# Values of two key tiles at a time, paired products in three pieces, and gathers one at a time in a fused attention and mixture-of-experts kernel

## The reference

```python
x = L0_attn_x                                   # (8, 512, 256)
xn = layernorm(x)
# attention, 16 heads of 16: each of q, k, v and the output is a low-rank projection
def holo_linear(x, basis, phase, amp):          # basis (32, 256), phase and amp (256, 32)
    return (x @ basis.T) @ (amp * cos(phase)).T
attn = softmax(q @ k.T * 16 ** -0.5); out = holo_linear(attn @ v, basis_o, phase_o, amp_o)
# feed-forward: 8 experts of width 352, the best 2 of each row, weighted, plus shared experts of width 704
y = sum_e combine[t, e] * (silu(xn @ w_gate[e]) * (xn @ w_up[e])) @ w_down[e]
y = y + (silu(xn @ sw_gate) * (xn @ sw_up)) @ sw_down
return x + out + y
```

## Time and profile before

| | us |
|---|---|
| median of 3 runs | 1055.94 |
| lowest, highest | 1054.34, 1062.08 |
| the profiled execution | 1056.45 |
| its span, first to last instruction | 1054.6 |
| TensorE busy in the span | 931.8 (88%) |
| VectorE busy | 646.0 (61%) |
| ScalarE busy | 568.1 (54%) |
| GpSimd busy | 327.9 (31%) |
| mean granted TensorE clock | 0.926 of full |

### The profile page before, as it was taken

One profiled execution on the slowest core, in us unless ns is written; L12 is line 12 of the kernel. 1 busy time (PEld: TensorE's weight loads), 2 busy tenths in 40 slices (PEclk: granted clock), 3 DMA queues, 4 the chain that ended last, 5 costly groups with the idle time before them and its releaser, 6 DMA issues.

```text
span 1054.6 us, 19404 instructions
## 1 busy us (share of the span) xinstructions
PE 931.8 (88%) x6519; PEld 624.2 (59%) x6520; DVE 646.0 (61%) x978; ACT 568.1 (54%) x892; POOL 327.9 (31%) x305
## 2 busy tenths in 40 slices
PE   5756999999999779898998998998997998998898
PEld 3446999999999624455454455444544544544546
DVE  7778644444434555765774874874875775785653
ACT  5756544444444335554663663663664664665563
POOL 2006422222222060351343253244235235135043
PEclk9856999999999856898998998998998999999899
DMA  9976454222222354445446545545465365453220
GB/s 317 377 253 191 137 164 115 73 71 70 70 70 66 94 146 127 124 119 147 126 117 174 151 111 166 147 129 142 133 154 154 108 169 134 138 122 77 48 63 21
DMA packets 94086, 140.02 MB, mean 133 GB/s; under 512 B 18200, under 2 KB 51488, under 8 KB 92992
## 3 DMA queue, kind: packets, MB, share of 16 engines
q1 hardware_dynamic: 87328, 121.25, 40.5%
q0 software_dynamic: 6480, 17.70, 5.7%
q10 hardware_dynamic: 208, 0.14, 0.0%
HBM read 79.24 MB, written 54.71 MB: 127 GB/s over the span
## 4 chain that ended last, share of the span: by engine, by line
PE 48%; issue 24%; POOL 11%; DVE 9%; ACT 3%; another core or an unknown queue 2%; DMA 2%; SPq 0%; POOLq 0%; ACTq 0%; DVEq 0%
PE bank L1253 7%; PE s_pair L1235 6%; PE st_pair L1235 6%; PE bank L1382 5%; PE bank L1444 4%; PE st_pair L1370 4%; POOL y_b L784 3%; PE bank L1348 3%; POOL h_T L767 3%; PE s_pair L1309 3%; DVE top L1773 2%; PE bank L1243 2%; PE bank L1218 2%; ACT prob L1031 1%
## 5 line engine op out<-in xcount | busy, mean ns | idle before, releaser
L1773 DVE TENSOR_REDUCE top<-s_pair 128x2 f32<-128x1024 f32 x252 | 308.5, 1224 | 144.0 <-PE s_pair L1309 122.7
L1031 ACT ACTIVATE prob<-st_pair 128x1024 f32<-128x1024 f32 x256 | 261.6, 1022 | 217.1 <-PE st_pair L1370 152.5
L767 POOL TENSOR_TENSOR h_T<-h_f,h_T 128x512 fp32r<-128x512 f32 x40 | 51.3, 1283 | 410.7 <-ACT h_T L1013 410.7
L1382 PE MATMUL bank<-prob,v_ones 128*32 128x512 f32 x1024 | 156.4, 637 | 4.6 <-issue 4.3
L745 POOL DMA_INDIRECT xg<-xn_rows,token_of x71 | 82.9, 1168 | 216.6 <-PE bank L1218 164.6
L1348 PE MATMUL bank<-xT_b,w_sh 64*128 64x512 f32 x960 | 129.5, 402 | 15.7 <-DVE h_f L1794 13.4
L1370 PE MATMUL st_pair<-q_rows,k_rows 50*128 50x512 f32 x512 | 126.3, 480 | 14.7 <-ACT prob L1031 7.5
L1309 PE MATMUL s_pair<-k_rows,q_rows 48*128 48x512 f32 x504 | 117.0, 450 | 14.4 <-DVE top L1773 7.4
L1370 PEld LDWEIGHTS st_pair<-q_rows,k_rows 50*128 50x128 f32 x512 | 51.0, 191 | 122.8 <-ACT prob L1031 78.0
L1348 PEld LDWEIGHTS bank<-xT_b,w_sh 64*128 64x128 f32 x960 | 91.1, 188 | 43.4 <-DVE h_f L1794 22.3
L1253 PE MATMUL bank<-w_exp,c_hT 128*128 (+1 forms) x639 | 94.2, 292 | 1.0 <-ACT c_y L957 1.0
(11 more groups left out here) (233 smaller groups left out, 1163.7 us busy)
## 6 DMA issues: line engine op xcount, KB each, us to landing
qk_rows<-qk_hi SPq DMA_DIRECT2D x56, 256.0 KB
q_rows<-qk_rows SPq DMA_DIRECT2D x64, 192.0 KB
k_rows<-qk_rows SPq DMA_DIRECT2D x56, 192.0 KB
expert_rows<-c_y SPq DMA_DIRECT2D x71, 128.0 KB, 1.7
xn_T_split<-x_T SPq DMA_DIRECT2D x8, 1024.0 KB, 6.5
xT_b<-xn_T_split SPq DMA_DIRECT2D x32, 256.0 KB
qk_rows<-qk_lo SPq DMA_DIRECT2D x28, 256.0 KB
x_all<-in_L_attn_x_dram SPq DMA_DIRECT2D x8, 512.0 KB, 8.1
```

The costliest lines, as they stand in the source:

```text
L767: pool.tensor_tensor(h_T[0:m, LO, f, :], h_f[q % 2][0:m, :], h_T[0:m, HI, f, :].bitcast(F32), ALU.subtract).then_inc(p_h, 1)
L1031: act.activation(prob[kt % 2][:, 2 * jp:2 * jp + 2, :].rearrange("p j l -> p (j l)"), st_pair[:, :], ACT.Exp, scale=HD ** -0.5).then_inc(a ...
L1382: ins = pe.matmul(ot_bank[32 * j:32 * j + 32, :], v_ones[:, kt, 4 * g + j, :], prob[kt % 2][:, j, :], start=(kt == 0), stop=(kt == TPB - 1))
L1773: dve.tensor_reduce(top[g % 2][:, :, jp, qt], score_pair(b, g, v)[:, :].rearrange("p (i k) -> p i k", i=2), AX_X, ALU.max).then_inc(d_max, 1)
```

## The change

- `values` runs for two key tiles in one burst: tiles 0 and 1 at step 4, tiles 2 and 3 at step 0 of the next slot. `prob` gets a third buffer in place of the third `xT` buffer.
- A block of the shared experts takes half a slot (`unit` by half, eight a batch). Its 24 matmuls go in three pieces of 12, 4 and 8 over the three steps after a burst (PIECES). A down unit now covers two output tiles, 68 matmuls in pieces of 28, 16, 18 and 6, the last in the step of the burst. `gate_up_both` and `low_rank_o` share one unit.
- In the steps without a burst the score comes before `score_T`; in those with one, after.
- `tanh`, the hidden product, `hidden_high`, the projections, `project_o`, the v values and `max_rows` move to other steps. `max_rows` comes at step 5, after the transposes behind the burst of step 4.
- Each gather waits for a step of its own in the first three slots of its batch, and the scaling starts after the eighth.
- With two `xT` buffers the rows are loaded twice: `load_xT` for the low rank and `load_xF` for the shared experts. `load_xF` waits until the batch's last product is done; it stands at the end of SP's fourth slot. SP's order within a slot changes.
- TensorE's waits for the shared bank `m_bank` are rewritten for the new order.

```diff
-        xT_2 = sb("xT_b2", [P, 2, KT, L], F32R, late)
-        prob = [sb(f"prob{i}", [P, 4, L], F32, late) for i in range(2)]
+        prob = [sb(f"prob{i}", [P, 4, L], F32, late) for i in range(3)]
...
-        xT_bs = [xT_b, xT_1, xT_2]
+        xT_bs = [xT_b, xT_1]
...
-        FIRST = 4
+        FIRST = 2
         ORDER = (0, SFT - 1) + tuple(range(1, SFT - 1))
         BOTH = 1
-        PROJECTED = [(0, 0), (0, 2), (1, 0), (1, 2)]
-
-        def unit(b, g, t):
-
-            if t % 2 == 0:
-                return None, None, None
-            u = g * 4 + t // 2
-            c, i = b if u >= FIRST else b - 1, (u - FIRST) % 16
-            if i == 3:
-                return ("out", c - 1, 0) if there(c - 1) else (None, None, None)
+        PROJECTED = [(0, 2), (0, 6), (1, 2), (1, 6)]
+
+        def unit(b, g, half):
+
+            u = g * 2 + half
+            c, j = b if u >= FIRST else b - 1, (u - FIRST) % 8
+            if j == BOTH:
+                return "odd", c, j
             if not there(c):
                 return None, None, None
-            if i < 3:
-                return (("first", c, 0), ("second", c, 0), ("both", c, BOTH))[i]
-            return (("first", "second")[i % 2], c, i // 2) if i < 12 else ("down", c, i - 12)
+            return ("pair", c, j) if j < SFT else ("down", c, j - SFT)
+
+        def unit_before(b, g, half):
+            return unit(b, g, 0) if half else unit(*after(b, g, -1), 1)
+
+        def for_rows(b):
+
+            return xT_bs[(b + 1) % 2 if b > 1 else 1]
+
+        def for_shared(b):
+
+            return xT_bs[b % 2]
...
+            def load_xF(b):
+                wait(sp, b_r, min(b + 2, NB))
+                wait(sp, b_gu, (b - 1) * SFT)
+                for a in (HI, LO):
+                    for k in range(KT):
+                        o = (a * KT + k) * L
+                        sp.dma_start(for_shared(b)[:, a, k, :].bitcast(F32), xT_dram[of(b)][:, o:o + L]).then_inc(xF_in, 16)
...
 
             def slot(b, g):
                 (pb, pg), (ppb, ppg), (nb, ng), (qb, qg) = after(b, g, -1), after(b, g, -2), after(b, g, 1), after(b, g, 2)
+                if there(qb) and (qb, qg) != (0, 0):
+                    load_rows(qb, qg)
                 if ppg % 2 and moved(ppb, ppg // 2):
                     load_inverse(ppb, ppg // 2)
-                if there(qb) and (qb, qg) != (0, 0):
-                    load_rows(qb, qg)
-                if g == 1 and there(b + 1):
-                    store_qk(b + 1, 2)
-                if there(b + 1) and g < 2:
-                    store_qk(b + 1, (0, 3)[g])
-                if g == 2 and there(b + 2):
-                    if b < 0:
-                        load_xT(b + 2, HI)
-                    load_xT(b + 2, LO)
-                if g == 3 and there(b):
-                    load_x_b(b)
                 if pg % 2 and moved(pb, pg // 2):
                     move_sums(pb, pg)
                     move_values(pb, pg)
+                if g == 2 and there(b + 2):
+                    load_xT(b + 2)
                 if g == 0 and there(b + 1):
-                    store_qk(b + 1, 1)
+                    store_qk(b + 1, 0)
+                if g == 1 and there(b + 1):
+                    store_qk(b + 1, 2)
+                if g == 2 and there(b - 1):
+                    store_out(b - 1, 0)
                 if g == 3 and there(b + 2):
                     store_low_rank(b + 2)
-                    load_low_rank(b + 2)
-                if g == 2 and there(b - 1) and b < NB:
-                    store_out(b - 1, 0)
                 if there(nb):
                     load_max(nb, ng)
                 if pg % 2 == 0 and moved(pb, pg // 2):
                     move_values(pb, pg)
                 if pg % 2 and moved(pb, pg // 2):
                     store_inverse(pb, pg // 2)
-                if g == 1 and there(b) and there(b + 2):
-                    load_xT(b + 2, HI)
-                if g == 2 and there(b - 1) and b < NB:
+                if g == 0 and there(b + 1):
+                    store_qk(b + 1, 1)
+                if g == 1 and there(b + 1):
+                    store_qk(b + 1, 3)
+                if g == 2 and there(b - 1):
                     store_out(b - 1, 1)
-
+                if g == 3 and there(b + 2):
+                    load_low_rank(b + 2)
+                if g == 3 and there(b):
+                    load_x_b(b)
+                    if there(b + 1):
+                        load_xF(b + 1)
...
-            def gather_batch(b):
-                if there(b):
-                    for n in range(4):
-                        gather_y(b, n)
-                    wait(pool, b_st, b * 32 + 4)
-                    for n in range(4, 8):
-                        gather_y(b, n)
-
-            gather_batch(0)
+            def gather_at(b, n, g, t):
+                wait(pool, b_st, b * 32 + g * 8 + t + 1)
+                gather_y(b, n)
+
             for b in range(NB):
-                hidden_low(b, 0)
+                gather_at(b, 0, 0, 4)
+                gather_at(b, 1, 0, 6)
+                gather_at(b, 2, 1, 0)
+                gather_at(b, 3, 1, 2)
                 if there(b - 1):
                     ao_low(b - 1, 1)
+                hidden_low(b, 0)
+                gather_at(b, 4, 1, 7)
+                gather_at(b, 5, 2, 1)
+                gather_at(b, 6, 2, 3)
+                hidden_low(b, 2)
+                gather_at(b, 7, 2, 6)
                 for n in range(4):
                     scale_y(b, n)
-                hidden_low(b, 2)
+                hidden_low(b, 3)
                 for n in range(4, 8):
                     scale_y(b, n)
-                hidden_low(b, 3)
+                ao_low(b, 0)
                 add_pair(b)
                 hidden_low(b, 4)
                 add_y(b)
-                ao_low(b, 0)
                 hidden_low(b, 5)
-                gather_batch(b + 1)
...
             def exponent(b, g, t):
                 kt, jp = t // 2, t % 2
-                if jp == 0:
-                    wait(act, b_pv, b * 16 + g * 4 + kt - 1)
+                n = b * 16 + g * 4 + kt
+                if jp == 0 and n >= 3:
+                    wait(act, b_pv, (n - 3) // 2 + 1)
                 wait(act, b_st, b * 32 + g * 8 + t + 1)
-                act.activation(prob[kt % 2][:, 2 * jp:2 * jp + 2, :].rearrange("p j l -> p (j l)"), st_pair[:, :],
+                act.activation(prob[n % 3][:, 2 * jp:2 * jp + 2, :].rearrange("p j l -> p (j l)"), st_pair[:, :],
                                ACT.Exp, scale=HD ** -0.5).then_inc(a_exp, 1)
 
...
+            PIECES = ((0, 6), (6, 8), (8, 12))
+            DOWN_PIECES = ((0, 14), (14, 22), (22, 31), (31, 34))
...
+            def down_pair(b, pair, piece):
+
+                first, end = DOWN_PIECES[piece]
+                if first == 0:
+                    wait(pe, d_dn, b * TPB + 2) if pair else wait(pe, d_hf, b * SFT + SFT)
+                if piece in (1, 3):
+                    pe.wait_ge(b_ha, swaps(b, SFT + 2 * pair) + 1 + piece // 2)
+                for m in range(first, end):
+                    n, i = DOWN_ORDER[m]
                     q, a, c = DOWNS[i]
...
 
+            def next_score(b, g, t):
+                (nb, ng), (qb, qg) = after(b, g, 1), after(b, g, 2)
+                if t < STEPS - AHEAD:
+                    if there(nb):
+                        score(nb, ng, t + AHEAD)
+                elif there(qb):
+                    score(qb, qg, t - STEPS + AHEAD)
+
+            def piece(b, g, t):
+                what, c, j = unit(b, g, t // 4)
+                n = t % 4 - 1
+                if n < 0:
+                    what, c, j = unit_before(b, g, t // 4)
+                    if what == "down":
+                        down_pair(c, j, 3)
+                elif what == "pair":
+                    gate_up_shared(c, j, n)
+                elif what == "down":
+                    down_pair(c, j, n)
+                elif what == "odd":
+                    if n == 0 and there(c):
+                        gate_up_both(c)
+                    if n == 2 and there(c - 1):
+                        low_rank_o(c - 1)
+
             def slot(b, g):
-                now, (pb, pg), (nb, ng), (qb, qg) = there(b), after(b, g, -1), after(b, g, 1), after(b, g, 2)
+                now, (pb, pg), (nb, ng) = there(b), after(b, g, -1), after(b, g, 1)
                 for t in range(STEPS):
+                    if t % 4:
+                        next_score(b, g, t)
                     if now:
                         score_T(b, g, t)
-                    if t < STEPS - AHEAD:
-                        if there(nb):
-                            score(nb, ng, t + AHEAD)
-                    elif there(qb):
-                        score(qb, qg, t - STEPS + AHEAD)
-
-                    if g == 3 and t == 2 and there(b + 2):
-                        low_rank(b + 2)
-                    if (g, t) in PROJECTED and there(b + 1):
```

(42 more changed lines are left out.)

184 lines of the change are left out of this document (104 added, 80 removed).

## The result

| | before | after |
|---|---|---|
| median, us | 1055.14 (4 runs) | 1079.34 (4 runs) |
| lowest, highest | 1049.34, 1062.08 | 1077.32, 1082.29 |
| ratio, 95% interval | | 1.0229 (1.0160 to 1.0298) |
| profiled execution, its span | 1056.45, 1054.6 | 1081.26, 1079.3 |
| mean granted TensorE clock | 0.926 | 0.924 |

The change made the kernel 2.3% slower. The forecast was 984, with a range up to 1018.

A forecast was written before the change was run, and what follows sets the result against it. TensorE was taken as the busiest engine, stalled 8.0 us per batch beside gathers. From 1056.45, 56 for stalls and 17.5 for bursts less 1.0 at the end (72.5) gave 984 us; 8-in-10 range 963 to 1018.

The forecast's parts named there:

- Period and stall of before: A batch pass takes 83.1 us: 75 of work and waits, 8.0 of TensorE stall beside eight gathers in a row.
- Gathers one at a time: Spacing each batch's eight gathers ends seven TensorE stalls of 8.0 us: gain 56, bounds 0 and 60.
- Bursts and pieces: Values in bursts and shared-expert products in pieces, with the extras, cut a batch from 75.0 to 72.5 us.
- The chains: Maximum (1.75 us) and exponential (1.57) through single buffers limit steps two and three; four steps sum to 8.07.
- the holes: TensorE idles about 0.8 us in step two and 0.4 in step three of every four.
- One slip in the sum: Hidden product ends 0.9 us after the burst; its piece, startable at .58, waits .37 unless transposes come first.
- The second load: Normalised rows loaded again on SP's queue, 1 MB more ahead of q and k rows: 0.3 us per batch.
- GpSimd's chain at nothing: Scaling starts after all eight gathers; 17 to 19 us of GpSimd work fits in over 25 before the down product.
- A: Rival: stalls go, but bursts give nothing or q and k rows come 2.5 us late per batch; 1000 to 1018; chance 0.17.
- B: Rival: the stalls stay because they come from DMA traffic, not the row of gathers; 1040 us; chance 0.09.
- C: Rival: TensorE's idle holes hold its clock down; 1074 us with half the slots at half clock; chance 0.06.
- a sign of being wrong by far: The prediction would be wrong by far if the clock of the batches fell below 0.95.

The follow-up runs named there:

- e14_spaced: The kernel before, with each of a batch's eight gathers waiting for a score step of its own; 1002.2 us, where before takes 1051.9.
- e11_all: The changed kernel with late q/k stores and column load moved behind the rows, and the residual's load ahead of the low rank's; 987.7 us, before 1051.9.
- e1_rows: The changed kernel with later q/k stores behind the next slot's row load and the column load behind slot 0's row loads; 1007.8 us, before 1014.3.
- e7_xF: The changed kernel with only the load of the shared expert's columns moved behind slot 0's loads of rows; 1059.2 us, where before takes 1017.3.
- e3_all: The same kernel as e11_all on another chip; 993.1 us, where before takes 1014.3.
- e18_shift: The kernel before with all eight gathers still in one row, let go at step 2 of slot 1; 1046.4 us, where before takes 1053.0.
- e13_four: The kernel before with its eight gathers in two rows of four, the second at step 7 of slot 0; 1040.8 us, where before takes 1051.9.
- e9_after: The changed kernel, unchanged, run again; 1081.8 us, where before takes 1051.5.

## Why the prediction was wrong, point by point

**Period and stall of before** (83.1 = 75 + 8.0): right, within 1 us. Spaced, six passes of e14_spaced (from ScalarE's timeline, every 32nd exponential) average 75.7 us; 75 was forecast. The stall was 7.1 instead of 8.0 (49.7 us over seven).

**Gathers one at a time, 56 us:** the mechanism right, the term a little large: 49.7. That the gain exists only on some chips could not be read from one profile.

**Bursts and pieces, 75.0 to 72.5:** right in kind. e11_all against e14_spaced, on one chip: 75.7 to 73.8 us per pass and 14.5 us in all, where 15.9 to 16.5 was forecast; on the other chip 9.3 (1002.3 to 993.1). The undisturbed pass is 73.3 (last row of e11_all's passes), 0.8 over the forecast. The chains are as drawn: 8.18 us for four steps in the changed kernel, from the score at 614.54 to 622.72, against 8.07. In e1_rows TensorE waits for the maximum 12.5 us in 37 times and for the exponential 9.1 in 39, so the holes are filled by the chains that were named. One slip in the sum is small: a product ready 0.9 after the burst that could start at 0.58 waits 0.32, not 0.37, 0.2 us per batch.

**The second load, 0.3 per batch (bounds 0 and 2.5):** this step failed. The sum was 8.4 to 9 us against 8.5 to 9. Measured: SP reached the load of columns only at 552.26, behind slot 3's moves of values, six loads of the low rank and the residual; the rows landed at 564.2, 11.9 us later; the score wanted them at 561.7, and would have at 559.4 without the 2.32 for h_T. In these 11.9 us 2.93 MB passed, where the sum had counted 1.84: the residual and the rest of slot 3's transfers, just issued, shared the time. The term was 22 us (e7_xF), 3 per batch, ten times what I took and over its bound. I had counted the two loads alone, not what stands ahead of them and passes with them, nor the half clock behind a wait; and the start itself rested on a wait for the last product that the code does not have.

**What is not in the prediction at all:** the two stores that the change moved behind SP's waits in slots 0 and 1. They are in the diff; they cost 46.5 us, half of the loss, in a term put at nothing without a reason. "The second load" asked what stands in front of the rows in slot 0 and left slots 1 and 2, which have the same rows behind another instruction. The question "what is queued behind the waiting instruction" was asked of the new load and not of the moved ones.

**GpSimd's chain at nothing, "slack of 25 us":** the slack was in its work and not in its inputs. o_b came 9.8 us late, since its load stood behind the low rank's on SP. Its price is 14.8 us (e1_rows to e3_all). That the last sum could hold up the down product was named as what would make the prediction wrong; its cause, the place of one load, was in the diff.

**Rivals.** A had the mechanism (rows late) at 2.5 us per batch in one slot; it was 14 in three slots (88 against 73.8), with h_T's. B is out: the same bytes pass when spaced, and the stall goes. The Trainium skill (DMA: Bandwidth & Descriptors, Issuing engines are not separate DMA queues) says that all issuers' transfers interleave on the same 16 engines. The runs don't contradict that, but the stall follows the row of gathers (e18_shift) and the chip, not the share (0.69 with it, 0.71 without). C came about in its effect and not by its cause: the clock was 0.94 in the passes, below the 0.95 named as a sign of being wrong by far, and fell after TensorE had stood waiting for the rows (0.56 from 610.13 to 614.00); with the holes alone e11_all's passes run at 1.00.

**The sum, mended:** 987.7 where 984 was forecast. So the forecast fits a kernel whose SP queue had been ordered for it. That it fits within 4 us is in part luck: the stall and the bursts gave 6.3 and 2.0 us less than forecast, and the sum started from 1056.45, where before takes 1051.9 beside e11_all. Where before takes 1014 the parts would have given 21 us (1014.3 to 993.1), not 72.5.

## What to carry to other kernels

When a change moves an instruction on a queue that waits in order, list for every slot what now stands behind its wait and when that is wanted; the price is the wait, the bytes put in front, and the half clock that follows. A faster engine makes every load's deadline earlier, so check the loads against the new period, not the old one. Space out indirect gathers (pairs, some steps apart, were enough), and do not trust one chip's profile for what an unbroken row costs.

## What the runs showed of the hardware that was not expected

- One program (before) takes 1051.5 to 1055.1 us on some chips and 1014.3 to 1017.3 on others, and most of the difference is in the stretches beside the row of gathers (20 matmuls in 8.03 us, or 90). The same kernel with spaced gathers takes 1002.2 and 1002.3.
- The stall holds TensorE, VectorE and ScalarE alike (4, 3 and 2 instructions in 3.5 us in e13_four), and can begin with the fourth gather of a row.
- After a wait of 3.24 us the burst of 16 took 3.22 us instead of 1.92; a wait for a DMA cost 5.1 where 3.24 stand in the list. Of the 94 us lost, 56 are listed waits of TensorE (44.2 for q_rows and 11.7 for h_T in e9_after); the rest was not split further, but the clock of the passes rose from 0.94 to 1.00 with them.
